# The queries' loop of a fused convolution and attention kernel: one repeated step, outputs finished per pair of tiles

## The reference

```python
x = x + L0(_gn(x), ...)      # per-image rotated 3x3 grouped convolution, then a channel gate
x = x + L1(_gn(x), ...)      # below

# L1, per image, N = 4096 tokens, C = 256, 8 heads of 32
q = xt @ Wq.T + bq;  kv = xt @ Wkv.T + bkv
q = (relu(q) + 1e-06) / scale          # k likewise
q_norm = norm(q);  q = q**3;  q = q / norm(q) * q_norm
z = 1 / (q . k.sum + 1e-06)
kv_state = einsum('bjc,bjd->bcd', k, v)
out = einsum('bic,bcd->bid', q, kv_state) * z
out = out + depthwise5x5(v)
out = out @ Wproj.T + bproj
```

## Time and profile before

| | |
|---|---|
| time, median of 3 runs | 4146.31 us (4144.97 to 4148.81) |
| time of the profiled execution | 4144.54 us, of which 4142.8 us are the span from first to last instruction |
| busy share of the span | PE 88%, DVE 72%, ACT 65%, POOL 34% |
| mean granted clock of PE | 0.975 of full speed |
| one pass of the batch loop (from 2231.2 to 2480.3 us) | 249.1 us |
| of it keys and values / depthwise / first layer | 64.0 / 33.6 / 50.0 us |
| of it queries: start, middle, end | 30.7 / 54.3 / 16.5 us |

### The profile page before, as it was taken

How to read it: one execution, slowest core, us unless ns; L and a number is a source line. 1 busy time by engine, 2 the same in 40 slices (tenths; PEclk the granted TensorE clock), 3 DMA queues, 4 the chain that set the end, 5 groups by cost and what they waited for, 6 DMA issues and landing times.

```text
span 4142.8 us, 94163 instructions
## 1 busy us (share of the span) xinstructions
PE 3626.4 (88%) x26496; PEld 2712.7 (65%) x26496; DVE 2962.9 (72%) x8401; ACT 2677.9 (65%) x7373; POOL 1395.2 (34%) x1317
## 2 busy tenths in 40 slices
PE   0469999899989989999989989989999989989998
PEld 0156776757668675776757668575776757667686
DVE  6466867768676776867768686776867678685766
ACT  2275766757577675767657577675767757577675
POOL 0441523325133241523325143242523325143311
PEclk9989999999999999999999999999999999999999
DMA  4435434344443435434344443535434344442512
GB/s 165 136 102 156 135 108 130 123 122 141 130 132 107 141 107 156 135 112 136 114 124 139 128 139 99 146 102 156 135 116 137 110 133 133 130 140 62 153 44 72
DMA packets 558468, 516.39 MB, mean 125 GB/s; under 512 B 97297, under 2 KB 491665, under 8 KB 557713
## 3 DMA queue, kind: packets, MB, share of 16 engines
q1 hardware_dynamic: 557968, 510.53, 40.8%
HBM read 351.02 MB, written 134.22 MB: 117 GB/s over the span
## 4 chain that ended last, share of the span: by engine, by line
PE 57%; DVE 20%; issue 12%; ACT 7%; DVEq 1%; DMA 1%; POOL 1%; SPq 1%; ACTq 0%; POOLq 0%
PE VAB L1262 11%; PE F L1281 10%; PE VAB L1281 6%; PE F L1320 6%; PE VAB L1320 5%; PE T L1292 4%; PE SM L1359 4%; PE VAB L1340 2%; PE T L1349 2%; DVE WK L837 2%; ACT WK L1083 2%; ACT WK L1077 2%; DVE XR L799 2%; DVE F L816 2%; PE F L1283 2%
## 5 line engine op out<-in xcount | busy, mean ns | idle before, releaser
L1281 PE MATMUL F<-WQ,XHL 128*128 128x256 f16 x6144 | 829.9, 277 | 46.6 <-DVE XR L799 13.7
L1262 PE MATMUL VAB<-WK,BD 128*128 128x512 f16 x3072 | 706.9, 386 | 85.1 <-DMA BD<-RHL 54.7
L528 POOL TENSOR_TENSOR XR<-XR,V 128x512 f32<-128x512 f32 x256 | 327.7, 1280 | 1213.3 <-DVE XR L890 1213.3
L1077 ACT ACTIVATE WK<-F,SCAL 128x256 f32<-128x256 f32 x1024 | 474.4, 470 | 379.6 <-DVE F L816 379.6
L511 POOL TENSOR_TENSOR WK<-XP,WK 128x1122 f16<-128x1122 f32 x128 | 289.9, 2265 | 1224.6 <-DVE WK L782 1224.6
L1281 PEld LDWEIGHTS F<-WQ,XHL 128*128 128x128 f16 (+1 forms) x6144 | 606.9, 100 | 130.2 <-issue 55.5
L1262 PEld LDWEIGHTS VAB<-WK,BD 128*128 128x128 f16 x3072 | 290.7, 98 | 466.3 <-DMA BD<-RHL 54.8
L1083 ACT ACTIVATE WK<-WK,SCAL 128x256 f32<-128x256 f32 x1024 | 512.8, 508 | 71.1 <-DVE WK L822 69.0
L816 DVE TENSOR_TENSOR F<-F,FL 128x512 f32<-128x512 f32 x512 | 354.9, 693 | 105.4 <-PE F L1283 103.6
L1281 PE MATMUL VAB<-WQ,XHL 128*128 128x256 f16 x3072 | 420.3, 279 | 0.0
L1154 ACT ACTIVATE XR<-XR,BPC 128x1024 f32<-128x1024 f32 x128 | 146.8, 1147 | 423.0 <-DVE ST L802 423.0
(11 more groups left out here) (185 smaller groups left out, 6897.6 us busy)
## 6 DMA issues: line engine op xcount, KB each, us to landing
XR<-xr SPq DMA_DIRECT2D x256, 512.0 KB, 5.0
XP<-xp SPq DMA_DIRECT2D x128, 561.0 KB, 3.8
x<-XR SPq DMA_DIRECT2D x512, 128.0 KB, 2.1
XP<-x SPq DMA_DIRECT2D x256, 256.0 KB, 3.4
XR<-x SPq DMA_DIRECT2D x256, 256.0 KB, 3.3
out<-XR SPq DMA_DIRECT2D x256, 256.0 KB, 3.0
BD<-RHL SPq DMA_DIRECT2D x256, 96.0 KB, 2.3
XHL<-toeplitz SPq DMA_DIRECT2D x2, 3072.0 KB, 13.0
```

The costliest lines, as they stand in the source:

```text
L528: g_.tensor_tensor(o, o, fm, ALU.add).then_inc(o_rdy, 2)
L1077: a.activation(K2[:, p, ts], F[p][:, ts], ACT.Square, scale=inv_a, accum_out=S2[:, 2 * p + t:2 * p + t + 1]).then_inc(f_sq, 1)
L1262: ins = t_.matmul(VA[q], BD[:, j, HALVES * wa + h, sx, P * sy:P * (sy + 1)], SG[:, g % 3, xa, 16 * q + sy:16 * q + sy + 16, sx:sx + 32], s ...
L1281: t_.matmul(o, XHL[:, xa, h, at], WQ[:, wa, h, c0:c0 + C], start=(k == 0), stop=False)
```

## The change

The queries' step is written in another order on PE, DVE and ACT, with the same instructions in it but for the output:

- DVE: `cube` is no longer called for the pair that `floor_max` of the same step has clamped. It is called first in the next step. `floor_max` stands last in the step.
- ACT: `sixths` of the pair ahead stands first, `squares` last.
- PE: `attention` stands first, then `output`, `transpose_o`, `project`, `transpose_q`.
- `output` works per pair: both channel halves of 256 tokens into one bank, pair 0 in PP and pair 1 in SM, 12 matmuls of 256 columns where a half had 6 of 512. It now follows in step s for pair s-4. `finish` handles one pair, both halves, in step s for pair s-4; before, the two halves of unit u were finished in steps 2u+6 and 2u+7, now its two pairs are in steps 2u+4 and 2u+5.
- `store` waits for both pairs of its unit before it writes either half.
- The first keys and values of the next image stand inside PE's `step_q`.

```diff
             def store(b, u):
                 for h in range(HALVES):
-                    sp.wait_ge(y_rdy, (b * NU + u) * HALVES + h + 1 + Y_CR)
+
+                    sp.wait_ge(y_rdy, b * PAIRS + 2 * u + 2 + Y_CR)
...
-            def finish(b, u, h):
-
-                dve.wait_ge(y_full, (b * NU + u) * HALVES + h + 1)
+            def finish(b, u, p):
+
+                m = b * PAIRS + 2 * u + p
+                dve.wait_ge(y_full, m + 1)
                 dve.wait_ge(r_in[u % 2], Y_OUT * (b * NU // 2 + u // 2 + 1))
-                r = R[:, u % 2, h, :, :].rearrange("p m n -> p (m n)")
-                v.scalar_tensor_tensor(r, (PP, SM)[h][:, :], out_fac, r, ALU.mult, ALU.add).then_inc(y_rdy, 1)
+                r = R[:, u % 2, :, :, 2 * HD * p:2 * HD * (p + 1)].rearrange("p h m n -> p (h m) n")
+                v.scalar_tensor_tensor(r, (PP, SM)[p][:, :].rearrange("p (a n) -> p a n", n=2 * HD), out_fac, r,
+                                       ALU.mult, ALU.add).then_inc(y_rdy, 1)
...
-            def step_q(b, u, p, live, nxt, keys=False, fresh=False):
+            def step_q(b, u, p, live, nxt, keys, keys_end, fresh):
                 n = b * 2 * PAIRS + PAIRS + 2 * u + p
+                if live(p - 1) or keys and p == 1 or keys_end and p == 0:
+                    cube(n - 1, 1 - p)
+                if live(p - 2):
+                    denominators(b, u - 1, p)
+                    inverses(b, u - 1, p)
+                    quotients(b, u - 1, p, fresh and u == 1 and p == 0)
                 if live(p - 4):
-                    low_out(b, u - 2, p)
+                    finish(b, u - 2, p)
+                if nxt:
+                    attn_input(b + 1, u - 3, p, False)
+                if live(p - 1):
+                    ratio(n - 1, 1 - p, S6, S2)
+                elif keys and p == 1:
+                    ratio(n - 1, 1 - p, S2, S6)
+                if live(p - 3):
+                    low_out(b, u - 2 + p, 1 - p)
                 if live(p) or keys:
                     floor_max(n, p)
-                if live(p - 1):
-                    ratio(n - 1, 1 - p, S6, S2)
-                elif keys:
-                    ratio(n - 1, 1 - p, S2, S6)
-                if live(-6):
-                    finish(b, u - 3, p)
-                if live(p - 2):
-                    denominators(b, u - 1, p)
-                if live(p) or keys:
-                    cube(n, p)
-                if live(p - 2):
-                    inverses(b, u - 1, p)
-                if live(p - 2):
-                    quotients(b, u - 1, p, fresh and u == 1 and p == 0)
-                if nxt:
-                    attn_input(b + 1, u - 3, p, False)
-                if keys and p == 1:
-                    scale_k(n - 1, 0)
+                if keys_end and p == 0:
+                    scale_k(n - 2, 0)
...
-            def output(b, u, h):
-                pe.wait_ge(ol_rdy, b * PAIRS + 2 * (u + 1) + OL_CR)
-                pe.wait_ge(y_rdy, (b * NU + u) * HALVES + h + 1)
-                k = 0
-                for kk in range(HALVES):
-                    for wa, xa in PASSES:
-                        ins = t_.matmul((PP, SM)[h][:, :], WP[:, wa, kk, h * P:(h + 1) * P],
-                                        OT[:, xa, kk, :].rearrange("p (y m x) -> p m y x", y=4, m=4),
-                                        start=(k == 0), stop=(k == 5))
-                        k += 1
+            def output(b, u, p):
+                m = b * PAIRS + 2 * u + p
+                pe.wait_ge(ol_rdy, m + 1 + OL_CR)
+                pe.wait_ge(y_rdy, m - 1 + Y_CR)
+                for h in range(HALVES):
+                    k = 0
+                    for kk in range(HALVES):
+                        for wa, xa in PASSES:
+                            ins = t_.matmul((PP, SM)[p][:, h * C:(h + 1) * C], WP[:, wa, kk, h * P:(h + 1) * P],
+                                            OT[:, xa, kk, 2 * P * p:2 * P * (p + 1)].rearrange(
+                                                "p (y m x) -> p m y x", y=2, m=4),
+                                            start=(k == 0), stop=(k == 5))
+                            k += 1
                 ins.then_inc(y_full, 1)
 
-            def step_q(b, u, p, live):
+            def step_q(b, u, p, live, nxt):
+
+                if live(p - 2):
+                    attention(b, u - 1, p)
+                if live(p - 4):
+                    output(b, u - 2, p)
+                if live(p - 3):
+                    transpose_o(b, u - 2 + p, 1 - p)
                 if live(p):
                     pe.wait_ge(f_cube, b * 2 * PAIRS + PAIRS + 2 * u + p + 1)
                     project(b, u, p, F, 0)
+                elif nxt and u == NU:
+                    keys(b + 1, 0, p)
                 if live(p - 1):
                     transpose_q(b, u - 1 + p, 1 - p)
```

More of the change, by code:

```diff
@@ L991, in batch @@
                     for p in range(2):
-                        step_q(b, u, p, alive(u), not last, not last and u == NU)
+                        step_q(b, u, p, alive(u), not last, not last and u == NU, not last and u == NU + 1, False)
             pixel_stats(0, True)
@@ L1130, in high_out, with step_q @@
                              ).then_inc(oh_rdy, 1)
[L1132 removed]
+            def step_q(b, u, p, live, nxt, keys, keys_end):
                 n = b * 2 * PAIRS + PAIRS + 2 * u + p
[L1134 to L1135 removed]
+                if live(p - 1) or keys and p == 1 or keys_end and p == 0:
+                    sixths(n - 1, 1 - p)
+                if nxt:
+                    attn_input(b + 1, u - 3, p)
+                if live(p - 3):
+                    high_out(b, u - 2 + p, 1 - p)
+                if live(p - 1):
+                    transposed_q(b, u - 1 + p, 1 - p)
+                    norms(n - 1, 1 - p, den_eps)
+                elif keys and p == 1:
+                    norms(n - 1, 1 - p, inv_a2)
                 if live(p) or keys:
                     squares(n, p)
[L1138 to L1149 removed]
             def shift(c, g):
@@ L1190, in batch @@
                     for p in range(2):
-                        step_q(b, u, p, alive(u), not last, not last and u == NU)
+                        step_q(b, u, p, alive(u), not last, not last and u == NU, not last and u == NU + 1)
             root(0, 0)
@@ L1368, in step_q @@
                     project(b, u, p, F, 0)
+                elif nxt and u == NU:
+                    keys(b + 1, 0, p)
                 if live(p - 1):
                     transpose_q(b, u - 1 + p, 1 - p)
-                if live(p - 2):
-                    attention(b, u - 1, p)
-                if p == 1 and live(-4):
-                    for h in range(HALVES):
-                        output(b, u - 2, h)
-                if live(p - 3):
-                    transpose_o(b, u - 2 + p, 1 - p)
+                if nxt and u == NU + 1:
+                    if p == 0:
+                        pe.wait_ge(o_rdy, 2 * PAIRS * (b + 1) + O_CR)
+                        carry(pe)
+                    values(b + 1, 0, p)
             def batch(b, ahead):
@@ L1412, in batch @@
                     for p in range(2):
-                        if not last and u == NU:
-                            keys(b + 1, 0, p)
-                        if not last and u == NU + 1 and p == 1:
-                            pe.wait_ge(o_rdy, 2 * PAIRS * (b + 1) + O_CR)
-                            carry(pe)
-                            values(b + 1, 0, 0)
-                        step_q(b, u, p, alive(u))
+                        step_q(b, u, p, alive(u), not last)
                         if not last and u == 0:
                             (group_mean, group_spread)[p](b + 1, 1)
-                if not last:
-                    values(b + 1, 0, 1)
             pe.wait_ge(ready, 1)
```

20 lines of the change are left out of this document (3 added, 17 removed).

## The result

The changed kernel takes 4585.76 us (median of 4 runs, 4580.49 to 4589.53). The kernel before, run beside it, takes 4147.56 us. The ratio is 1.1055, interval 1.1036 to 1.1074: 10.6% slower. The forecast had the sign and both of its waits; a third cost, a slower cast on DVE, it did not have. The time is 86 us above its 4500 and inside its range.

What follows compares the result with a forecast made beforehand. No engine is full; a loop between engines bounds each step. Middle +23.9, start +2.4 and +2, end -4.9: +23.4 us per pass, +351 over 15 passes, +5 for the last; +356 on 4144.5 gives 4500, range 4290 to 4600.

Steps and rivals of the forecast that it cites:

- both of its waits: DVE waits before `cube` for ACT's squares, and before `finish` for the residual's DMA; chance of both 62%.
- The gap: On DVE nothing stands between `floor_max` and `cube`, 1.95 us apart; costs 1.35 us per step, making it 5.86 us.
- The residual: SP's late load makes DVE's `finish` wait 2.75 us in five steps per pass; a round takes 14.47 us.
- The cast: In DVE's step the next image's cast was counted at 0.33 us, within the 5.86 us step.
- The order on PE, the pairs, `high_out`: PE's 4.6 us of work hides under the step; output per pair costs nothing; the wait for `high_out` goes.
- Start and end: Per pass, the start costs +2.4 us (steps 4 to 6) and +2 (steps 1 to 3); the end gives -4.9.
- The residual in time: Rival: residual loads land before `finish` asks, middle only +10.2 us per pass, time 4295; chance 16%.
- PE's clock fell: Rival: PE's clock halves after waits in the middle, `floor_max` about 1 us late per unit, +75 us, 4575; chance 14%.
- The rival on the faster side: Gap hidden, steps bounded by PE's 4.6 us of work, -134 us in all, time 4010; chance 4%.

Runs made afterwards that it cites:

- run with both edits: Changed kernel with the residual loaded before the next image's unit, and `finish`, cast and `low_out` put between `floor_max` and the next `cube`: 4276.59 us, ratio 1.0321.
- run with the residual ahead: Changed kernel, but SP loads the residual of unit u+2 before it waits for the next image's unit: 4405.89 us, ratio 1.0625.
- cast moved: Changed kernel with the residual loaded first and DVE's cast moved from ahead of `ratio` to behind `low_out`: 4325.72 us, ratio 1.045.
- run with `finish` one pair later: Changed kernel with residual loaded first, gap filled, PE's `output` last in the step, and `finish` handling pair s-5: 4021.96 us, ratio 0.9719.
- run with only the pairs: Kernel before with only `output`, `finish` and `store` per pair, `finish` of pair s-4 behind the cast, SP's list untouched: 4503.70 us, ratio 1.0879.
- three of the experiments: Apparently the three misses: gap filled with residual late, 4671.84 us; both edits with `output` ahead of `attention`, 4494.47; both edits with `output` last, 4272.52.

## Why the prediction was right, and where it was short

**The gap: right in kind and in its own size.** `cube` starts 1.95 us after `floor_max` with nothing between. The forecast wanted some 256 waits of 1.3 us; there are 272 with 343.1 us in sum, in the middle 1.26 us each. The run with both edits takes most of it away, but it also shows that filling a gap is worth what it opens only until the next loop: 1.25 us of the freed time came back as a wait of `floor_max` for PE.

**The residual: right, 10% too small.** 75 waits as counted, 3.02 us each instead of 2.75. The round again, by the forecast's terms: `finish` to the next `quotients` 5.15 us (5.19 forecast), from there to POOL's end 3.82 (3.33), from POOL's end to `finish` 6.73 (5.95). POOL ends later because its input waits for the slow cast. The last stretch is 2.16 us to SP's issue, 0.73 to the issue of the second half, 3.8 to its landing and 0.03 to `finish`; I had 2.00, 0.65 and 3.3. The 3.3 was the median of both halves. `finish` waits for the later one, and that one lands later when the next image's loads go ahead of it: 3.8 us after its issue in the median of these 75 (3.1 to 5.4), and 3.7 already in the kernel before. Without such loads ahead it is 3.2 to 3.3. The Trainium skill's page DMA: Bandwidth & Descriptors, by whose fixed cost of 2.0 us alone the time would have been some 98 us under my forecast, is further off than the row. I had left out the second part of its fit, which was made for DMAs that GpSimd issues: bytes over 436 GB/s, 0.6 us for these 256 KB. With it the estimate from the page is 2.6 us, still short of both. Its advice in the section Rules for kernel authors, to issue early and wait late, is what the run with the residual ahead bears out.

**The cast: the step that failed.** The forecast put "cast 0.33" into the step as its row had it. There the cast began 0.26 us before POOL's addition; with `finish` between `quotients` and cast it begins after it, and then takes 1.03 us. The kernel before had shown this elsewhere: 25 of its 256 casts, outside the middle of the loop, began while a POOL instruction had 0.3 us or more to run; they took 0.67 to 1.34 us, and each ended 0.28 to 0.29 us after POOL did. One of them stands at the end of the pass that the forecast read:

```profile
2476.07 1.09 POOL L519 TENSOR_TENSOR XHL<-XP,XHL 128x512 f16<-128x512 f32 x1 [0.59 <-DVE XHL L810]
...
2476.77 0.67 DVE L810 CAST XHL<-XP 128x512 f16<-128x512 f32 x1
```

With the 0.12 us by which it also comes late (2678.10 + 0.67 to 2678.89) an undisturbed step is 6.55 us and not 5.86. Six such steps in the middle of a pass by 0.69, and five rounds with 0.37 more than forecast in each late step (8.98 in the pass shown, instead of 8.61 us), are 6.0 us; the middle was 5.8 us above the forecast. Over 15 passes that is 87 us; start and end together give 10 of it back, the last pass adds 4 (+9 where I had +5), and the median lies 5 us above the profiled execution: the 86 us. A duration of an instruction that shares something with another engine holds only for the neighbours it had.

**The order on PE, the pairs, `high_out`: right.** Output per pair cost nothing, the wait before `low_out` fell from 105.2 to 0.8 us, and attention first is covered.

**Start and end: right in sum.** +4.6 for the start (forecast +4.4) and -5.8 for the end (-4.9). The start's sum is right by luck: its two parts were off by -0.8 and +1.0 us. The end gained more because the pass that I had read ended sooner than most: its 16.46 us from the last `floor_max` to the next keys are 17.12 in the mean of the kernel before. In the pass shown the last `values` begin 7.21 us after the last `floor_max` (2734.66); 7.2 was forecast.

**The rivals.** The residual in time did not happen; the run with it ahead gives that case its price, 4405.89 us, where I had 4295. Of the 111 us between, 80 are the cast (4325.72 with the cast moved); the other 31 I did not take apart. PE's clock fell, to 0.87 in the middle (1.00 in the earlier trace rows), and `output` after a wait of 1.53 us took 2.74 us for 12 matmuls, at a granted clock of 0.50, instead of 1.47 at 1.00. The Trainium skill's page TensorE: Matmul & The Clock Gate, section HAM oscillation, describes such bursts at half rate after waits, and the trace agrees. But no price of it shows in the steps: `floor_max` waited 99.2 us for PE over the whole kernel (103.6 before) and `denominators` 0.7. PE had that time over. Its +75 us, which would have come near the measured time, would have been right for a wrong reason. At the end of a pass, where the next `keys` wait for POOL, a lower clock can be seen too:

```profile
2739.23 1.35 PE L1279 MATMUL F<-WQ,XHL 128*128 128x256 f16 x6 [0.74 <-POOL XHL L520]
```

Six matmuls of the first keys in 1.35 us where the earlier trace rows has 0.83; the whole `project` then takes 2.85 us instead of 1.52 in this pass. But the change did not bring this. Such a first group of six takes over 1 us in 5 of the 15 passes of the changed kernel (1.13 to 1.46), and in 5 of the 15 before (1.03 to 1.46); the pass of the earlier trace rows is one of the others.

The rival on the faster side was a gap hidden by other work. The change does not hide it; the run with `finish` one pair later does, and gives 4021.96 us where that rival's sum was 4010.

**What stays open.** The run with only the pairs was 124 us above my estimate. Its rows say where its 363 us above the kernel before are (profiled executions): 255 before `finish` for the DMA, 33 more there for PE, 128 more before `cube`, 19 more before `floor_max`, and 65 less before `low_out`. That the 128 come of the place that `finish` left is read from the rows and was not tested by a run. Of the 187 us that remain when the residual is ahead and the cast moved (4325.72 against 4139.12 us), the empty gap is the cause that the profile names (343.9 us of waits before `cube`), with the shorter end and `high_out` against it, but no run filled the gap without moving `low_out` too.

## What to carry to other kernels

In an in-order queue, look for a pair of instructions with a trip to another engine between them, and count what stands in the gap: a reordering that empties it can cost the trip in every step (here 1.26 us of waiting), and one that fills it must not put there anything that may be late. Before pulling a consumer ahead, find the queue that its data comes through and what stands in front of it there; here one swap in SP's list was worth 180 us after the change and nothing before it. And when one loop is opened, read off the next one before hoping for its time: three of the experiments gave theirs to a wait one place further on, and it took the residual, the gap, `output` and `finish` together to turn 10.6% slower into 2.8% faster.

## What the runs showed of the hardware

A DVE cast from f32 to f16 within the on-chip memory, 0.42 us for 512 columns, takes 1.02 to 1.03 us when it starts while a POOL addition is under way, and ends 0.28 to 0.29 us after that addition (2837.23 against 2836.95; 2679.92 against 2679.63). Its end keeps to POOL's and not to its own start. In the changed kernel all 105 casts that begin 0.52 to 0.65 us after POOL's addition end 0.28 to 0.29 us after it; and so do the 25 of the kernel before, which begin 0.10 to 0.74 us after another POOL instruction. So it is not slowed, it waits; as 0.28 us is less than the 0.42 of a whole cast, a part of it seems to be done before, which no row shows. The Trainium skill's page SBUF — State Buffer, section Who interferes with whom, says the same: a DVE operation in a mode with two ports and a GpSimd operation exclude each other, and the one that was issued first holds the ports to its end. That this cast runs in such a mode no row here shows. In the other order, cast first, the cast takes its 0.42 us, and of the 0.16 us that by the same rule POOL's addition would be held up, begun 0.26 us after the cast, hardly anything shows: its median is 1.28 us there, and 1.27 us in the changed kernel, where it begins first. `finish`, which ran beside the same POOL addition (2678.10 to 2678.84), kept its 0.74 us, and so did all 149 that overlap one (0.74 to 0.75 us); one of its inputs lies in PE's output banks.

Of the residual's two transfers, the last two of four that SP issues in a row, the second lands 3.8 us after its issue in the median (75 times, 3.1 to 5.4), and `finish` starts 0.02 to 0.10 us after that. The second transfer of the 53 pairs without the next image's loads ahead has 3.3 us.
